# Flamingo block with two gated layers: layer 0's gate accumulates in the score banks, in two halves at two places

## The reference

```
Q = x Wq_c,  K = ctx Wk_s,  V = ctx Wv_s ;  char2sub = softmax(Q K^T / 16) V          # 512 x 256, "forward"
Q2 = ctx Wq_s, K2 = x Wk_c, V2 = x Wv_c ;  sub2char = softmax(Q2 K2^T / 16) V2
sub2char = interpolated from 1601 rows to 512                                         # "back"
gate = sigmoid([char2sub, sub2char] Wg^T + bg)
x = x + tanh(g) * (gate * char2sub + (1 - gate) * sub2char)
```

## Time and profile before

| | us |
|---|---|
| median of 3 runs | 1392.84 |
| lowest and highest | 1389.47, 1395.42 |
| span of the profiled execution | 1388.3 |
| TensorE busy / ScalarE / VectorE / GpSimd in it | 1323.2 / 736.2 / 779.2 / 478.3 |

### The profile page before, as it was taken

The page is one execution under the profiler, slowest core; times in us unless marked ns, Lnnn a source line. Parts: engine busy times, 40 slices in busy tenths (PEclk is TensorE's granted clock), DMA queues, the critical chain, the costliest instruction groups (busy, mean ns, idle before and its releaser), DMA issues. The chain is left out here.

```text
span 1388.3 us, 25467 instructions
## 1 busy us (share of the span) xinstructions
PE 1323.2 (95%) x9828; PEld 1239.0 (89%) x9828; DVE 779.2 (56%) x1736; ACT 736.2 (53%) x1405; POOL 478.3 (34%) x378
## 2 busy tenths in 40 slices
PE   6999999999989999999999998899999999999996
PEld 5987969969759999999998998899999879999996
DVE  6566686776865535435444323666876774466322
ACT  4464555455554655555555554454554546567544
POOL 0100001001026656556465443111201246667544
PEclk9999999999999999999999999999999999999999
DMA  6102031220235545455363334112312166565322
GB/s 225 61 12 92 16 128 46 67 86 7 84 85 159 123 83 148 93 116 146 63 150 54 56 59 88 46 59 70 128 35 92 47 219 159 131 163 127 53 52 40
DMA packets 73675, 127.48 MB, mean 92 GB/s; under 512 B 7952, under 2 KB 53664, under 8 KB 73504
## 3 DMA queue, kind: packets, MB, share of 16 engines
q1 hardware_dynamic: 46816, 81.92, 17.9%
q0 software_dynamic: 26688, 43.34, 16.9%
HBM read 100.44 MB, written 24.79 MB: 90 GB/s over the span
## 5 line engine op out<-in xcount | busy, mean ns | idle before, releaser
L2551 DVE TENSOR_TENSOR m_hidden_lo<-m_act_out,m_hidden_hi 128x512 fp32r<-128x512 f32 x224 | 154.9, 693 | 353.6 <-ACT m_hidden_hi L2491 343.2
L434 PE MATMUL banks<-m_down_hi,m_hidden_hi 128*128 128x256 f32 x896 | 258.5, 288 | 1.4 <-DVE m_hidden_lo L2551 0.9
L434 PE MATMUL banks<-m_down_lo,m_hidden_hi 128*128 128x256 f32 x896 | 255.8, 286 | 2.4 <-issue 2.4
L434 PE MATMUL banks<-m_down_hi,m_hidden_lo 128*128 128x256 f32 x896 | 255.8, 285 | 0.0
L434 PE MATMUL banks<-m_xt_hi,m_up_hi 128*128 128x256 f32 x640 | 184.1, 288 | 1.4 <-DVE m_xt_lo L2534 1.4
L434 PE MATMUL banks<-m_xt_hi,m_up_lo 128*128 128x256 f32 x640 | 180.8, 282 | 0.0
L434 PE MATMUL banks<-m_xt_lo,m_up_hi 128*128 128x256 f32 x640 | 180.6, 282 | 0.0
L434 PEld LDWEIGHTS banks<-m_down_hi,m_hidden_hi 128*128 128x128 f32 x896 | 172.2, 192 | 4.6 <-DVE m_hidden_lo L2551 1.1
L434 PEld LDWEIGHTS banks<-m_down_lo,m_hidden_hi 128*128 128x128 f32 x896 | 172.2, 192 | 2.6 <-issue 2.6
L434 PEld LDWEIGHTS banks<-m_down_hi,m_hidden_lo 128*128 128x128 f32 x896 | 172.0, 192 | 0.0
L2491 ACT ACTIVATE m_hidden_hi<-m_act_out 128x512 fp32r<-128x512 f32 x224 | 141.6, 632 | 7.1
(11 more groups left out here) (387 smaller groups left out, 3430.5 us busy)
## 6 DMA issues: line engine op xcount, KB each, us to landing
stage<-in_up SPq DMA_DIRECT2D x22, 512.0 KB, 5.0
stage<-in_down SPq DMA_DIRECT2D x21, 512.0 KB, 4.0
stage<-in_ctx_rows SPq DMA_DIRECT2D x20, 512.0 KB, 4.3
stage<-in_ctx_cols SPq DMA_DIRECT2D x24, 402.0 KB, 3.3
m_stage<-in_down SPq DMA_DIRECT2D x10, 512.0 KB, 5.2
m_stage<-in_up SPq DMA_DIRECT2D x9, 512.0 KB, 4.8
rows<-xn SPq DMA_DIRECT2D x8, 528.0 KB, 3.7
stage<-in_ctx_picked SPq DMA_DIRECT2D x8, 512.0 KB, 4.6
```

The costliest lines, as they stand in the source:

```text
L434: mm = q.e.matmul(dst, a, b, start=first and n == 0, stop=last and n == 2, skip_group_check=True)
L2551: q.e.tensor_tensor(lo, m.act[(n * HP + h) % ACTS], f32(hi), ALU.subtract).then_inc(*hidden_lo.mark((layer, n, h)))
```

## The change

The gate's sums move from two ring banks to the score banks 2 and 3 (`gate_bank`). `tensor_gate` is split in two calls. The first, with the forward values, stands behind the next batch's queries (in the last batch behind two `tensor_put`) and ahead of `tensor_turn_pc`; it waits for the exponentials that still read banks 2 and 3. The second, with `s2c`, stands where the gate stood, with k as the outer loop, each k waiting for one copy. The last back mix marks its first half, on which the first `s2c` copy now waits. The next batch's first scores wait for the tanh before they write banks 2 and 3. `stay_busy` goes in batches 0 to 2, and falls from 18 to 6 matmuls in batch 3.

```diff
@@ tensor_scores, for c in range(CHUNKS)
+                if layer == 0 and i == 0 and c >= KD:
+                    q.wait_ge(*gate_out.of(b - 1, c - KD))
@@ tensor_turn_pc
-            if j == 0:
-                stay_busy(q, bank, 6 if b + 1 < BATCH else 18)
+            if j == 0 and b + 1 == BATCH:
+                stay_busy(q, bank, 6)
@@ tensor_back_mix, for m in range(KD)
+                if j == TT - 1 and m == 0:
+                    mm.then_inc(*back_mixed.mark((b, "half")))
@@ scalar_back_mix
-            q.wait_ge(*back_mixed.of(b, TT - 1))
             q.wait_ge(*turned_pc.of(b, TT - 1))
             for m in range(KD):
+                q.wait_ge(*back_mixed.of(b, TT - 1 if m else "half"))
                 act_high(q, ("s2c", b, m), a0.s2c[:, m, :], ps[:, m, :], col("bv_c", m))
@@ tensor_gate
-        def tensor_gate(q, b):
-            banks = []
-            for m in range(KD):
-                use = ("gate", b, m)
-                bank, emptied = gen.take(use, gate_out, (b, m))
-                q.wait_ge(*emptied)
-                banks.append(bank)
+        def gate_bank(m):
+            return ps[:, KD + m, :]
+
+        def tensor_gate(q, b, f0):
+            src = a0.s2c if f0 else a0.cv
             q.wait_ge(*gate_weights_in.of("gate"))
-            for src, f0 in ((a0.cv, 0), (a0.s2c, KD)):
-                q.wait_ge(*(his.of("s2c", b, KD - 1) if f0 else his.of("cv", 0, b, KD - 1)))
-                for m in range(KD):
-                    for k in range(KD):
-                        mm = q.e.matmul(banks[m], a0.gate_w[:, f0 + k, m * P:(m + 1) * P], src[:, k, :], start=f0 + k == 0,
-                                        stop=f0 + k == 2 * KD - 1, skip_group_check=True)
-                    if f0:
-                        mm.then_inc(*gate_in.mark((b, m)))
+            for m, k in [(m, k) for k in range(KD) for m in range(KD)] if f0 else [(m, k) for m in range(KD) for k in range(KD)]:
+                q.wait_ge(*(his.of("s2c", b, k) if f0 else his.of("cv", 0, b, k)))
+                if f0 == 0:
+                    q.wait_ge(*back_exped.of(b, 1, KD + m))
+                mm = q.e.matmul(gate_bank(m), a0.gate_w[:, f0 + k, m * P:(m + 1) * P], src[:, k, :], start=f0 + k == 0,
+                                stop=f0 + k == 2 * KD - 1, skip_group_check=True)
+                if f0 + k == 2 * KD - 1:
+                    mm.then_inc(*gate_in.mark((b, m)))
@@ tensor_attention_0
+                tensor_gate(q, b, 0)
                 tensor_turn_pc(q, b, 0)
                 tensor_turn_pc(q, b, 1)
...
-                tensor_gate(q, b)
+                tensor_gate(q, b, KD)
```

More of the change, by code:

```diff
@@ L1275, in scalar_gate @@
                 q.wait_ge(*gate_in.of(b, m))
-                q.e.activation(a0.work[:, m, :], gen.of(("gate", b, m)), ACT.Tanh, bias=half_bg[:, m:m + 1], scale=0.5).then_inc(
+                q.e.activation(a0.work[:, m, :], gate_bank(m), ACT.Tanh, bias=half_bg[:, m:m + 1], scale=0.5).then_inc(
                     *gate_out.mark((b, m)))
```

## The result

| | before | after |
|---|---|---|
| median of the runs, same chip | 1393.99 (1389.21 to 1397.24, 6 runs) | 1375.87 (1374.38 to 1378.59, 6 runs) |
| ratio, 95% interval | | 0.9881 [0.9857, 0.9904] |
| span of the profiled execution | 1388.3 | 1372.7 (own time 1375.1) |
| from the start of a batch's last query record (batch 3: of the puts behind the queries) to the next scores (batch 3: the experts' first block) | 19.53, 19.97, 19.91, 21.73 | 16.18, 16.81, 16.81, 19.40 |

What follows compares the result with a forecast made beforehand. TensorE, busy in nearly every slice of the attention, was taken as the bound. Batch gains of 2.8 + 2.9 + 2.9 + 2.4 made 11.0 us, taken off the median 1392.84: 1381.8 us, whole range 1377.5 to 1390.

Steps and rivals of the forecast that it cites:

- Forward half ahead of the turning: Gate's forward half before the turned probabilities, batch 0: no wait, 2.38 of its 3.43 us free, turning 1.05 us late.
- Mix 2 pays for the delay: Third back mix's wait for a ScalarE copy absorbs the 1.05 us: 0.98 in batch 0, some 0.55 left over in 1 and 2.
- The gate waits 0.65 in batch 0: Gate's other half waits 0.65 us because ScalarE converts late-landing context rows before the first mix copy; bounds 0 and 1.05.
- Batch 3: Last batch: turning 0.85 to 0.9 us late, unabsorbed; 3.43 saved at the gate, first copy costs 0 to 0.2; 2.4 gained.
- No wait at chunks 2 and 3, the body stays at 72.4: Next batch's score chunks have 2.0 and 2.3 us slack for the tanh, so TensorE's following work isn't delayed.
- The clock: TensorE's granted clock: no change expected from removing fillers; the rival that it falls had 8%, named at 1402 us.
- the clock stays at 1.00 up to 396: Sign that would confirm the forecast: TensorE's granted clock holds the 2.4 GHz level up to 396 us.
- Sum of the attention: Gains over the four batches, 2.8 + 2.9 + 2.9 + 2.4, together 11.0 us off the profiled span of 1388.3.
- Removed:* the fillers ... Nothing more: Claimed the edit removes only fillers of batches 0 to 2 and two `gen` takes per batch; no further effect.
- Behind the attention each wait is for work of the same chain, so nothing takes it back: After the attention, later stages keep the whole 11.0 us gain.
- my rivals: Three: delay not absorbed, 1385.2 (18%); next batch takes gain back, 1389 to 1392.8 (12%); clock falls, 1402 (8%).

Runs made afterwards that it cites:

- before without fillers: The kernel before with its filler matmuls ahead of the turning cut, 6 to 0 in batches 0 to 2 and 18 to 6 in batch 3: 1395.37, single run.

## Why the forecast was right and wrong

- *Forward half ahead of the turning*: right. No wait, 2.38 us filled, turning 1.05 late (102.25 net of the start).
- *Mix 2 pays for the delay*: right in batch 0, where its wait of 0.98 is gone. In batches 1 and 2 I left 0.55 over, which makes 2.9; the ends gave 3.15 and 3.10. That is 0.2 us too careful each.
- *The gate waits 0.65 in batch 0*: wrong, it waited 0. The rows' transfer was sent 0.8 us later net of the start, but the piece was converted at 110.91 - 1.54 = 109.37, against 109.56. The lower bound of the prediction held. End: 3.35 instead of 2.8.
- *Batch 3*: 2.33 for 2.4. The turning came 0.98 late for 0.9 at most. I had put the wait at the second bank; the trace has it at the first, for the exponential one tile earlier. The sum is nearly the same: the wait at the first bank moves the second bank to 365.33, behind the exponential that it needs (364.43 + 0.69).
- *No wait at chunks 2 and 3, the body stays at 72.4*: right. The body of batch 2 was even 0.28 shorter.
- *The clock*: right for the change, 1.00 in both windows. The sign "the clock stays at 1.00 up to 396" failed at 37.5 us, ahead of all that was changed. The Trainium skill ("TensorE: Matmul & The Clock Gate", Part 1) has the throttled clock as the default and activity as what releases it; before without fillers agrees, with 0.55 behind the wait of 2.31 us in batch 0, though not behind the same wait in batches 1 and 2.
- *Sum of the attention*: 11.0 forecast, 12.2, 11.9 and 12.2 in three pairs of profiles, 10.2 and 13.9 by the ratios with the length restored. Batch 0's 0.65 us for the rows is the term that was off most.

**The step that failed** is "*Removed:* the fillers ... Nothing more", and with it "Behind the attention each wait is for work of the same chain, so nothing takes it back". The second half of that holds, but I asked only whether a later stage could lose the gain, and none of my rivals had the time falling there. The edit also removed 59 instructions from TensorE's list, and with them 5.3 us of a slow branch, idle time and low clock 340 us later (3.3 to 5.3 over all profiles). The stall came back in every repeat of before, stayed away in every repeat of after, and was brought back by 59 instructions that do nothing. The row of the stall stood in the trace of before, at 740.23 with "issue" as its releaser; the earlier trace rows ended at 400 us. A wait that nothing in the profile explains, in code behind the edit, should have widened the range by its own length on both sides: 3.3 us lower, its end would have been 1374.2, below the measured 1375.87.

## What to carry to other kernels

Put work that is ready ahead of a wait in place of fillers, and check which later wait on the same engine absorbs the delay: here 3.43 us of matmuls brought 3.1 to 3.4 us in three batches and 2.3 in the last. Before a small change is judged by its time, pad the shorter program to the length of the longer one with instructions that stay in it, and compare both traces landmark by landmark, branches included; a difference that appears in a stage without an edit is no merit of the edit, and the next edit can take it away.

## What the runs showed of the hardware

- TensorE can stand 3 us in the middle of ready work, with the length of the program as the only thing changed. Its compare-and-branch at that place takes 2.94 to 3.59 us in the seven profiles with the stall and 0.35 in the nine without; the median of that line's 54 branches is 0.07 us. In five of the seven the clock falls behind it, in before to a mean of 0.55 over 3.8 us. The length cost 6.0 us by the ratios of the timed runs, of which the profiles tie 3.3 to the stall.
- An instruction that only raises a semaphore takes 0.15 us of TensorE's list: 59 end at 9.7 us and are hidden by the wait for the first weights, 128 run until 20.2 us and delay the first matmul from 9.99 to 20.47 us.
- The clock fell behind two of the four waits that lost their fillers, of 2.31 and 3.63 us, and cost 0.5 and 1.4 us, but not behind the other two, of 2.31 us each.
- Chips differ: two gave before medians of 1390.7 and 1394.7 us, two others 1401.6 us and, in a single run, 1404.2.
